# Layer 0 of a CIN tower: the last 40 pairs stacked for one f32r pass, the next rows turned two groups later, quad 3 laid out first, early additions in three more tiles

## The reference

```python
e = stack([tbl_f[ids[:, f]] for f in range(39)], axis=1)          # 512 x 39 x 16
def _cin_layer(X0, Xi, W, b):                                     # H = 128
    return einsum('hjk,bjd,bkd->bhd', W.reshape(H, F0, Fi), X0, Xi) + b[None, :, None]
Xi, res = e, []
for W, b in ((W0, b0), (W1, b1), (W2, b2)):
    Xi = _cin_layer(e, Xi, W, b)
    res.append(Xi.sum(axis=2))
h = concatenate(res + [dense_ctx], axis=1)
h = relu(h @ W_top1 + b_top1); h = relu(h @ W_top2 + b_top2); y = h @ W_top3
```

## Time and profile before

| | |
|---|---|
| median of three runs | 683.49 us |
| the profiled execution's own time | 684.21 us |
| its span in the trace | 682.3 us |
| mean granted TensorE clock | 0.995 |
| PE busy | 664.0 us (97%) |
| ACT busy | 567.3 us (83%) |
| DVE busy | 512.4 us (75%) |
| POOL busy | 443.4 us (65%) |

### The profile page before, as it was taken

One profiled execution on the slowest core, in us unless ns is written; L12 is line 12 of the kernel. 1 busy time (PEld: TensorE's weight loads), 2 busy tenths in 40 slices (PEclk: granted clock), 3 DMA queues, 4 the chain that ended last, 5 costly groups with the idle time before them and its releaser, 6 DMA issues.

```text
span 682.3 us, 10404 instructions
## 1 busy us (share of the span) xinstructions
PE 664.0 (97%) x2702; PEld 491.7 (72%) x2702; DVE 512.4 (75%) x984; ACT 567.3 (83%) x1997; POOL 443.4 (65%) x437
## 2 busy tenths in 40 slices
PE   4899999999999999999999999999999999999998
PEld 4766776677777777777777777777777777776683
DVE  5687887687787778777877787787878777888680
ACT  3586978798888888898988889888989898998672
POOL 6658374887778877788787777887788556333000
PEclk9899999999999999999999999999999999999899
DMA  6231234232423333333312212131313141005200
GB/s 211 77 96 9 56 58 120 38 98 11 153 40 110 85 94 99 68 98 68 97 8 77 29 38 65 13 90 5 98 7 98 5 139 37 0 1 184 116 1 1
DMA packets 107533, 46.04 MB, mean 67 GB/s; under 512 B 80897, under 2 KB 92941, under 8 KB 107474
## 3 DMA queue, kind: packets, MB, share of 16 engines
q1 hardware_dynamic: 101427, 42.82, 23.8%
q0 software_dynamic: 5120, 1.29, 2.2%
q10 hardware_dynamic: 927, 1.26, 0.7%
HBM read 13.81 MB, written 5.24 MB: 28 GB/s over the span
## 4 chain that ended last, share of the span: by engine, by line
PE 83%; ACT 1%; issue 1%; POOL 1%; DVE 0%; DMA 0%; SPq 0%; ACTq 0%; DVEq 0%; POOLq 0%
PE ps_y L995 19%; PE ps_y L997 18%; PE ps_y L996 18%; PE ps_x L910 12%; PE ps_g L1012 4%; PE ps_tr L879 1%; PE ps_y L1058 1%; PE ps_y L1056 1%; PE ps_y L1057 1%; ACT prod L611 1%; PE ps_y L1070 1%; PE ps_y L1006 1%; PE ps_tr L887 1%; PE ps_tr L900 1%; POOL room L423 1%
## 5 line engine op out<-in xcount | busy, mean ns | idle before, releaser
L611 ACT ACTIVATE prod<-ps_y,xt 128x128 f32<-128x128 f32 x1792 | 493.9, 431 | 75.2 <-PE ps_y L997 67.4
L995 PE MATMUL ps_y<-w_hi,x_hi 128*128 128x512 f32 (+1 forms) x640 | 312.8, 489 | 5.2 <-DVE prod L802 2.5
L996 PE MATMUL ps_y<-w_lo,x_hi 128*128 128x512 f32 (+1 forms) x640 | 249.6, 390 | 0.0
L997 PE MATMUL ps_y<-w_hi,x_lo 128*128 128x512 f32 (+1 forms) x640 | 249.5, 390 | 0.0
L428 POOL TENSOR_TENSOR prod<-prod 128x512 f32<-128x512 f32 x112 | 144.5, 1291 | 99.5 <-ACT prod L611 97.5
L802 DVE SCALAR_TENSOR_TENSOR prod<-ps_y,xt,prod 128x128 f32<-128x128 f32 x576 | 165.0, 344 | 45.1 <-PE ps_y L997 44.7
L399 POOL DMA_INDIRECT rows<-in_table,index x160 | 154.1, 963 | 49.6 <-issue 26.5
L809 DVE TENSOR_REDUCE prod<-prod 128x128 f32<-128x1536 f32 (+1 forms) x64 | 120.6, 1884 | 65.7 <-ACT prod L611 65.7
L995 PEld LDWEIGHTS ps_y<-w_hi,x_hi 128*128 128x128 f32 x640 | 120.8, 189 | 58.6 <-issue 24.6
L996 PEld LDWEIGHTS ps_y<-w_lo,x_hi 128*128 128x128 f32 x640 | 121.0, 189 | 48.5 <-issue 25.0
L423 POOL TENSOR_TENSOR room<-room 117x512 f32<-117x512 f32 (+1 forms) x105 | 135.2, 1290 | 24.2 <-DMA room<-room 21.4
(11 more groups left out here) (120 smaller groups left out, 329.1 us busy)
## 6 DMA issues: line engine op xcount, KB each, us to landing
room<-room SPq DMA_DIRECT2D x75, 234.0 KB
room<-room SPq DMA_DIRECT2D x45, 78.0 KB
emb_room<-rows SPq DMA_DIRECT2D x168, 5.0 KB
rows<-in_table,index POOLq DMA_INDIRECT x160
w_hi_dram<-g_all SPq DMA_DIRECT2D x5, 512.0 KB, 4.3
w_lo_dram<-g_all SPq DMA_DIRECT2D x5, 512.0 KB, 5.1
room<-room SPq DMA_DIRECT2D x15, 156.0 KB
g_all<-in_L_rec_W SPq DMA_DIRECT2D x9, 256.0 KB, 6.0
```

Source lines behind the costliest of these rows:

```text
L611: ins = nc.scalar.activation(prod[:, SLOT[k] + m // 2, :, m % 2], ps_y[:, g % YBANKS, m * H:(m + 1) * H], ACT.Copy, scale=xt[:, q % 2, ti, ...
L995: nc.tensor.matmul(y, hi, w1_hi[:, cols], start=True, stop=False)
L996: nc.tensor.matmul(y, hi, w1_lo[:, cols], start=False, stop=False)
L997: nc.tensor.matmul(y, lo, w1_hi[:, cols], start=False, stop=True).then_inc(y_made, 1)
```

## The change

Four edits go together.

1. **Chunks.** `xa` gets a fourth part of 11 rows, so chunks 0 to 3 use 128, 127, 126 and 125 rows, chunks 4 and 5 keep 117, and 40 pairs are left (`LAST`, `LEFT_ROWS`), cut as four runs of 10 rows on either side (`RUNS`, `load_runs`: eight DMAs). Chunks 1 to 3 are cut in two DMAs each. Chunk 1 has a semaphore of its own (`first_cut`).
2. **The last chunk stacked.** From quad 4 on ACT rounds the 40 products to f32r (`split_last`), DVE takes the rest, SP stacks high, high and low under each other (`stack`, two DMAs), and PE does one f32r matmul of 120 rows with the weights stacked high, low, high.
3. **Places.** Rows are turned after (2, 6) and kept after (2, 7); quad 3's after (2, 9) and (3, 0). The sums' and the products' tables change. In SP's pass for quad 2 the rows of quad 3 are laid out ahead of the eight run DMAs.
4. **Additions.** POOL also adds in tiles 3, 4 and 7 (`ADDED_EARLY`), and `reduce_early` reads 1536 elements there too.

```diff
+STEP = 6
+CHUNKS = STEP + 1
+LAST = STEP
+EXTRA, EXTRA_CHUNKS = 21, 4
+RUN = 10
+RUNS = [(11, 29), (11, 30), (11, 31), (11, 32)]
+LEFT_ROWS = RUN * len(RUNS)
-MULTIPLIED_IN = {(0, 0): [2], (0, 1): [3], (1, 0): [4], (1, 1): [5], (2, 0): [6]}
+MULTIPLIED_IN = {(0, 0): [2], (0, 1): [3], (1, 0): [LAST], (1, 1): [4], (2, 0): [5]}
-TURNED_AFTER, KEPT_AFTER = (2, 4), (2, 6)
+TURNED_AFTER, KEPT_AFTER = (2, 6), (2, 7)
-THIRD_TURNED_AFTER, THIRD_KEPT_AFTER = (3, 1), (3, 3)
-SUMMED_AFTER = {(0, 2): 0, (0, 5): 1, (0, 8): 2, (1, 1): 3, (1, 8): 4, (2, 8): 5, (3, 2): 6}
-THIRD_SUMMED_AFTER = {(0, 4): 0, (0, 7): 1, (0, 9): 2, (1, 2): 3, (1, 8): 4, (2, 8): 5, (3, 2): 6}
+ADDED_EARLY = [3, 4, 7]
+THIRD_TURNED_AFTER, THIRD_KEPT_AFTER = (2, 9), (3, 0)
+SUMMED_AFTER = {(0, 2): 0, (0, 8): 1, (1, 1): 2, (1, 8): 3, (2, 5): 4, (3, 0): 5, (3, 2): LAST}
+FOURTH_SUMMED_AFTER = {(0, 4): 0, (0, 7): 1, (0, 9): 2, (1, 2): 3, (1, 8): LAST, (2, 8): 4, (3, 2): 5}
 SECOND_SUMMED_AFTER = {(1, 9): 0, (2, 1): 1, (2, 3): 2, (2, 5): 3, (2, 7): 4, (3, 0): 5, (3, 2): 6}
+STACKED_FROM = 4
+SPLIT_LAST_AFTER = (1, 9)
-GATHERED_AT = {2: [0, 8, 9, 11, 13, 15, 17], 3: [0, 0, 0, 0, 42, 44, 46, 48, 50, 52],
+GATHERED_AT = {2: [0, 8, 9, 11, 13, 15, 17], 3: [0, 0, 0, 0, 38, 40, 42, 44, 46, 48],
...
+            def load_runs(q, landed):
+                if q - 1 >= STACKED_FROM:
+                    sp.wait_ge(z_lo_made, q - STACKED_FROM)
+                else:
+                    sp.wait_ge(z_used, CHUNKS * (q - 1) + summed(q - 1).index(LAST) + 1)
+                for n, (l, r) in enumerate(RUNS):
+                    at = slice(RUN * n, RUN * (n + 1))
+                    sp.dma_start(left[at, :], x0[l:l + RUN, q % 2, :]).then_inc(landed, 16)
+                    sp.dma_start(bz[at, LAST, :], x0[r:r + RUN, q % 2, :]).then_inc(landed, 16)
...
             for q in range(1, QUADS):
                 sp.wait_ge(x0_made, q + 1)
                 share_rows(q, shared[q % 2])
-                for c in range(1, CHUNKS):
+                cut_window(q, 1, first_cut[q % 2])
+                for c in range(2, LAST):
                     cut_window(q, c, cut[q % 2])
+                if q != 2:
+                    load_runs(q, runs_ld[q % 2])
                 if q + 1 < QUADS:
                     lay_out(q + 1)
+                if q == 2:
+                    load_runs(q, runs_ld[q % 2])
...
+                if q >= STACKED_FROM:
+                    stack(q)
...
+            def split_last(q):
+                act.wait_ge(z_made, CHUNKS * q + multiplied(q).index(LAST) + 1)
+                if q > STACKED_FROM:
+                    act.wait_ge(z_used, CHUNKS * q)
+                nc.scalar.copy(z_stack[0:LEFT_ROWS, :], bz[0:LEFT_ROWS, LAST, :]).then_inc(z_hi_made, 1)
...
+                if ti == SPLIT_LAST_AFTER[0] and STACKED_FROM <= q + 1 < QUADS:
+                    n = q + 1 - STACKED_FROM
+                    dve.wait_ge(z_hi_made, n + 1)
+                    wait(dve, z_stacked, 32 * n)
+                    nc.vector.tensor_tensor(z_low, bz[0:LEFT_ROWS, LAST, :], z_stack[0:LEFT_ROWS, :].bitcast(F32),
+                                            ALU.subtract).then_inc(z_lo_made, 1)
                 if ti == 1 and q + 1 < QUADS:
                     spread(q + 1)
...
+                if c == LAST and q >= STACKED_FROM:
+                    pe.wait_ge(w0_stacked, 32)
+                    pe.wait_ge(z_stacked, 32 * (q - STACKED_FROM + 1))
+                    w, z = w0_stack[:], z_stack
```

More of the change, by code:

```diff
@@ L130, in chunk_rows, with window_parts, share_parts @@
 def chunk_rows(c):
-    return F * sum(c + CHUNKS * a < SHIFTS for a in range(SPC))
+    return LEFT_ROWS if c == LAST else P - c if c < EXTRA_CHUNKS else REP
+def window_parts(c):
+    n = chunk_rows(c)
+    return [(0, REP)] + ([(REP, n)] if n > REP else [])
+WINDOWS = sum(len(window_parts(c)) for c in range(2, LAST))
+def share_parts():
+    return [(F * a, F * (a + 1), -STEP * a % F) for a in range(SPC)] + [(REP, P, EXTRA)]
 def build(nc, dense_ctx, ids, bases, table, W_top1, b_top1, W_top2, b_top2, W_top3, W0, b0, W1, b1, W2, b2, out):
@@ L321, in _ @@
             sp.wait_ge(x0_made, 1)
-            for a in range(SPC):
-                share_rest(sp, a)
-            for c in range(1, CHUNKS, 2):
+            for part in share_parts():
+                share_rest(sp, part)
+            for c in range(1, LAST, 2):
                 cut_rest(sp, c)
+            for n, (l, r) in enumerate(RUNS):
+                at = slice(RUN * n, RUN * (n + 1))
+                sp.dma_start(left[at, P:], x0[l:l + RUN, 0, P:]).then_inc(first_runs, 16)
+                sp.dma_start(bz[at, LAST, P:], x0[r:r + RUN, 0, P:]).then_inc(first_runs, 16)
             def load_w2(n):
@@ L479, in _ @@
                 gather_behind(3, g)
+            add_groups(3, 0)
+            add_groups(3, 1)
             repeat_rows(2)
-            for g in range(4, 8):
+            for g in range(4, 7):
                 gather_behind(3, g)
+            add_groups(4, 0)
+            gather_behind(3, 7)
+            add_groups(4, 1)
+            gather_behind(3, 8)
             multiply(2, 0)
-            for g in range(8, GATHERS):
-                gather_behind(3, g)
+            gather_behind(3, 9)
             multiply(2, 1)
@@ L491, in _ @@
                 multiply(2, 3 + g)
-            multiply(2, 6)
+            repeat_rows(3)
             for g in range(3, 5):
                 gather_behind(4, g)
-            repeat_rows(3)
-            for g in range(5, 9):
+            multiply(2, LAST)
+            for g in range(5, 7):
                 gather_behind(4, g)
+            add_groups(7, 0)
+            gather_behind(4, 7)
+            add_groups(7, 1)
+            gather_behind(4, 8)
             multiply(3, 0)
@@ L585, in _ @@
             act.wait_ge(first_xa_moved, 1)
-            nc.scalar.copy(xa[0:REP, 0:P], ps_g[0:REP, 0:P]).then_inc(first_xa, 1)
+            nc.scalar.copy(xa[:, 0:P], ps_g[:, 0:P]).then_inc(first_xa, 1)
             nc.scalar.copy(rest, turned[:, :, 1:, :]).then_inc(x0_made, 1)
             act.wait_ge(x0_made, 1)
-            for c in range(2, CHUNKS, 2):
+            for c in range(2, LAST, 2):
                 cut_rest(act, c)
```

187 lines of the change are left out of this document (123 added, 64 removed).

## The result

The changed kernel takes 676.72 us (median of seven runs, 676.39 to 681.33), beside 683.48 for the kernel before on the same chip (seven runs, 682.2 to 684.36): ratio 0.9918, 95% interval 0.9894 to 0.9941. The forecast was 681.2, so the direction was right and the gain, 6.8 us and not 2.3, was three times as large. The profiled execution took 677.4 us, its span 674.6. All ratios here leave out five single executions that took 829 us or more: one each of b128, b127, a_nostack, a_turn4 and of the kernel before beside b128.

What follows compares the result with a forecast made beforehand. PE was taken as the bound, without gaps in the steady state. Terms -7.6 + 0.6 + 0.6 + 2.0 + 1.6 - 0.6 - 1.1 + 0.8 + 2.8 - 1.4 = -2.3 took the median from 683.5 to 681.2 us; range 674.5 to 686.5.

Steps and rivals of the forecast that it cites:

- rival 1: SP's small copies are cheap, 0.45 us each, and quads 0 to 2 lose next to nothing: 675.8 us; chance 0.27.
- The stacked pass: Quads 4 to 15: last chunk as one f32r matmul, 0.23 us instead of 0.86, 12 times: -7.6 us.
- `sum_d`: Steady quads, tile 2: cover before `reduce_late` is used up, 0.05 us of PE waiting per quad, 12 quads: +0.6 us.
- Rival 3: DVE waits for ACT's copy and `sum_d` for DVE in every steady quad: +7.2 us, 688.4; chance 0.10.
- The turn: Steady quads: four turns leave from ahead of `sum_d`, their 0.78 us carried along; no change of price forecast.
- Tile 0: DVE's last product 2.0 us later behind SP's DMAs at 0.68 each: +2.0 us; slow clock after PE's stop: +1.6.
- rival 2: SP's small copies are dear, 0.91 us each; a documented rule gives 0.92: 685.7 us; chance 0.12.
- W0's five copies: Start: five more copies of W0's columns on DVE that PE waits for, 0.12 us each: +0.6 us.
- Quad 1: Chunk 1's product stops waiting for all six cuts; PE's 0.46 + 0.16 before 53.47 goes: -0.6 us.
- Quad 2's last chunk: Its eight run DMAs stand behind quad 3's layout, so PE waits: +2.8 us; separately, quad 3's turn: +0.8.
- Tile 8: PE's early waits: 1.0 of the 1.39 us at 115.33 kept, none of 0.74 at 121.67 or 0.3 behind: -1.4.
- Additions: Tiles 3, 4, 7: shorter `reduce_early` removes PE's wait for DVE at 84.31, behind tile 4: -1.1 us.

Runs made afterwards that it cites:

- b128: The kernel before with the turned rows 128 columns wide, not 123; 686.01 us beside 691.58, ratio 0.9915.
- b127: The kernel before with the turned rows 127 columns wide; 691.61 us beside 691.58, ratio 0.9997.
- a_nostack: The changed kernel without any stacked pass, all quads using the 40-row fp32 last chunk; 692.58 us beside 691.58 for the kernel before, ratio 1.0019.
- a_turn4: The changed kernel with rows turned behind group 4 of tile 2 again and kept behind group 6; 689.10 us beside 691.61 for the kernel before, ratio 0.9967.
- (8): The changed kernel with VectorE's subtraction for the stack moved from tile 1 to behind group 2 of tile 2; 685.49 us, ratio 1.0049 to the kernel before.
- again: The changed kernel unaltered, measured once more on a second chip; 677.41 us beside 681.65 for the kernel before, ratio 0.9929.
- a_q2late: The changed kernel with quad 2's last chunk summed behind group 5 of tile 7, not group 2; 675.91 us, ratio 0.9918 to the kernel before.
- best2: The changed kernel with some early run DMAs issued by ScalarE and quad 0's `spread` ahead of VectorE's last product; 680.63 us beside 691.61, ratio 0.9838.
- a_noadd: The changed kernel without GpSimd's additions in tiles 3, 4 and 7; 680.03 us, ratio 0.9965 to the kernel before.

## Why the prediction was right and where it failed

**The number.** 676.7 lies inside the stated range of 674.5 to 686.5, but outside the forecast's own 678.5 to 684. It is nearest to rival 1's 675.8, and rival 1's mechanism is out (a small DMA at 0.717 and not 0.45), so the number alone would have pointed at the wrong theory. By the table the spans differ by 7.7 and not 2.3. Of the 5.4 between them 3.1 lie ahead of tile 1's group 8, 1.6 between tile 12 and 56, 1.0 between tile 6 and 12 and 1.6 behind tile 63; 1.4 between tile 1 and 6 and 0.5 behind tile 56 go against them. The forecast failed in two places, the turn and tile 0, and errors of the other sign hid part of it.

**The stacked pass: right.** Forecast 0.63 a quad; the distance from tile 2 to tile 3 went from 9.07 to 8.45. ACT's copy took 0.61, DVE's subtraction 0.68, as read off.

**`sum_d`: right.** 0.05 a quad forecast; tile 1 to 2 takes 9.61, and 9.54 in a_nostack, which has no subtraction: 0.07. Rival 3 is out. That the subtraction is cheap where it stands, though, rests on what GpSimd does there (8).

**The turn: the step that failed in the steady state.** The prediction moved "the turn ... (-0.78)" and took its price along. The diff made it 128 columns wide, and the earlier trace rows was no longer its row. b128 alone gives 0.31 a turn, 3.4 us between tile 12 and 56 and about 4 in all by the trace, 5.6 by the medians. That this is near the 4.5 that the median lacked is in part chance, since tile 0 brought some 3 more and the next terms took as much away.

**Terms that were not there, of the other sign.** The 40-row fp32 chunk costs 0.4 more in quads 1 to 3, 1.2 us. In tile 5 PE waits for chunks 2 and 3 of quad 2, because GpSimd waits for SP's longer row of cuts: tile 5 to 6 takes 12.39 where it took 11.19, so 1.2 (in again 0.6, in a_q2late 0.3). From quad 8 on VectorE is late for a bank now and then, 1.4 us to tile 56, and 0.5 in quad 14, where the turn is missing and PE comes early. Between tile 12 and 56: -6.9 (stack) -3.4 (turn) + 0.8 (`sum_d`) + 1.4 = -8.1; measured -8.0.

**Tile 0: the DMA price right, its consequence wrong.** SP's ten-row DMAs took 0.717 each beside 0.68 forecast; rivals 1 and 2 are out, and the line's 0.92 with rival 2. SP was through at 36.6 (36.9 forecast). But the last one had landed 1.3 later and not 2.0, so the last product ended 1.05 later and not 2.0, and PE stopped for 1.66 at the chunk and 0.55 at the turn behind it, not for 2.8 in front of tile 1 (in again it stopped 0.29 at the turn and 1.21 in front of tile 1). A slow stretch did follow, 3.4 us from about 40 on, as forecast (+1.6). What the forecast did not have is that the one of the earlier trace rows would be missing, behind a stop of 1.08 where there had been 1.54. The two cancel. W0's five copies (+0.6) took some 0.1 each, as said, but tile 0's first matmul comes at 26.80 where it came at 27.42 (27.45 in again), so no delay by them is seen. Up to group 8 of tile 1 the forecast was +4.2; measured is +1.0, in again +0.8.

**Quad 1: right.** Forecast -0.6; tile 1 to 2 takes 12.26 where it took 12.78. The prediction's 0.16 of it has no row.

**Quad 2's last chunk: right in its place and cause, and dearer.** Forecast 2.8 of waiting and 0.8 at the turn; measured 2.18 and 0.30, in again 2.9. No slow stretch was forecast here, and one came: 1.7 us, in again 3.4. In a_q2late and best2, with waits of 0.94 and 0.44 there, it is absent.

**Tile 8: better than forecast.** 1.0 of the wait at 115.33 was kept; both waits, 1.39 and 0.74, are gone. Between tile 6 and 12 some 0.8 of the gain isn't accounted for by any of these terms.

**Additions: right.** 1.1 forecast, 1.4 by a_noadd.

**The run's own share.** 1.6 us of the two profiles' difference lie behind tile 63 and are the clock's.

## What to carry to other kernels

When an edit changes a size by a few columns or rows, every instruction that has it as an operand needs a new price, even one that the edit only moves: here a constant that looked like bookkeeping, 123 to 128, was worth about half of the main idea. Look for what a padded size buys: 128 columns in a float32 transpose, more than 40 rows in a float32 matmul. And before an elementwise instruction with both inputs in SBUF is moved on VectorE, read what GpSimd does at its new place, and what stands behind the DMA that waits for it.
